# Filter tables of the later layers on VectorE, a merged score product for the first query tile, and an order from measured durations

## The chip, the cores and the metric

The kernel runs on one core of a Trainium2 chip. The metric is the device time of one execution in microseconds (us), the median of three runs. The engines of the core work side by side, each through its own list of instructions in order, and wait for each other at semaphores: TensorE (PE: matmuls, and PEld: its weight loads), VectorE (DVE), ScalarE (ACT), GpSimd (POOL) and SyncE (SP, which here issues DMAs).

## What is computed

The input is 2048 tokens of 512 features (8 sequences of 256). Four residual blocks follow each other:

```python
x = x + attn_a(layernorm(x))   # 4 layers: norm, silu, long convolution with a
                               # complex exponential filter, norm, 64->256->64 MLP
x = x + ffn(layernorm(x))      # 512 -> 1792 -> 512, weights w * (su @ sv), silu gate
x = x + attn_b(layernorm(x))   # 32 query heads, 8 key heads of 128, causal, ALiBi
x = x + ffn(layernorm(x))
```

The filter of the convolution is a power series. It is computed as a rotation by an angle that grows with the position, held in tables of cosine and sine (`rot`), between which a running sum (a scan along time) is made:

```python
p = jnp.tanh(r) * jnp.exp(1j * jnp.angle(phazor_c))
prog = p[None, :] ** jnp.arange(L, dtype=jnp.float32)[:, None]
```

The attention of one key head and its four query heads is

```python
scores = jnp.einsum('bkgqd,bksd->bkgqs', qg, k) / math.sqrt(HD)
attn = jax.nn.softmax(scores + bias[None], axis=-1)   # bias: causal mask and slope * distance
```

## The kernel before

Everything is kept in float32 precision by splitting: a value is held as a high part in the reduced type `float32r` and a low part, the rest. A product is made of three matmuls (`PASSES`: high x high, high x low, low x high), in the helper `mm3`, whose matmul is line 624. All split products of the kernel therefore stand at line 624, and are told apart by the names of their tiles.

**Opening and first feed-forward block (phase 1).** The four blocks of 512 tokens ("stacks" s = 0 to 3) go through the four-layer convolution stack. Stack 0 is the lead: the feed-forward block can only begin with its result. One norm of a layer is a chain over all engines: `sq` (ScalarE), `var` (TensorE, line 1337), `eps` (VectorE, line 1183), `rstd` (GpSimd, `srstd`, line 810), `rtr` (TensorE, line 1346), `yn` (VectorE). Then `silu` (ScalarE, line 949), `ur` (VectorE, 1197) and `ui` (GpSimd, 818) multiply by cosine and sine, `zr` and `zi` are the scans (VectorE, 1208), `pr` (VectorE) and `pi` (GpSimd, 821) multiply by the tables again, and `conv` is TensorE's (1356, 1358). The projection into the stack is `proj` (line 1330), ahead of it `row`, `xT`, `xc` bring in and transpose the tokens. Folding steps prepare constants: `b1f` (line 1309), `boutf` (line 1314).

The tables are made by doubling: `turn k` (five instructions on GpSimd, lines 767 to 773) squares the rotation, and the table of 2^k positions becomes one of 2^(k+1). For layer 0 this is `tab0` on VectorE (lines 1092, 1094). For layers 1 to 3 it is `tabs` on GpSimd: three instructions (lines 790, 791, 793), for levels 0 to 4 all three layers in one, from level 5 (`TAB_EACH`) on each layer by itself, 14 tables in all. `ui` and `ur` of layer l wait for its tables.

The order of all instructions of phase 1 is made by a planner, `Steps.ordered`: each step has an engine, an expected duration in us, the steps that it needs, and an urgency (0 is the lead's). It places the step that can start first; up to 130 us (`PATIENT`) steps that would delay a lead step are held back. The last feed-forward block has an order of its own from the same planner (`order3`).

**Attention (phase 2).** 64 units, one for each of 8 key heads and 8 sequences, in the order written out in `order2`. A unit has four heads. TensorE computes the scores of the four heads (`sc`), then keys and values of the next unit (`kv`), transposes the probabilities of heads 0 and 1 (`pT`, line 1850), computes queries of the next unit (`q`), the product with the values (`at`), and so on. Scores of the first 128 queries reach 128 keys, those of the second 128 reach 256; both lie in one PSUM bank of 512 columns (`PART`: 0 to 128 and 128 to 384). VectorE adds the bias and takes the row extreme in one instruction (line 1758), ScalarE takes the exponential (1618), VectorE the reciprocal of its sum (`rsum`, 1765), GpSimd multiplies (1673). Each head's reciprocal stands behind the scores of the next head in VectorE's list. `biased` has two buffers, so that head n waits for the exponentials of head n-2. In the last unit of a key head, `alibi` (line 1708) makes the bias of the next one between the heads. In the first four units VectorE also does layer-norm statistics ahead of the scores; near the end one unit has four of them.

## Time and profile before

| | |
|---|---|
| three timed runs | 2542.87, 2538.52, 2543.79 us, median 2542.87 |
| the profiled execution | 2549.18 us, its span 2547.9 us, mean granted clock 0.981 |
| TensorE busy | 2481.8 us, 97% of the span |
| VectorE, ScalarE, GpSimd busy | 1284.1, 944.2, 669.1 us |
| chain of work that ended last | TensorE 95%, VectorE 2%, GpSimd 2%, ScalarE 1% |

The busy shares are means over stages that differ. TensorE's busy time counts overlapping instructions, so the pace of matmuls is read from start to start.

### The profile page before, as it was taken

What the parts mean: (1) busy time and instruction counts of PE and PEld (TensorE: products, weight loads), DVE (VectorE), ACT (ScalarE), POOL (GpSimd) and SP (SyncE); (2) the same over time, 40 slices, a digit from 0 to 9 for tenths busy, and PEclk for the clock granted to TensorE, in tenths of its full rate; (3) what the DMA queues carried; (4) which work ended last, traced back from release to release, by engine and by line L of the source; (5) the groups of instructions that cost most, each with busy time, mean ns of one, the idle gap of its engine ahead of it and who ended that gap; (6) DMA issues with size and microseconds to landing.
All of it is one profiled execution on the core that took longest, in us unless ns stands there. A gap on an engine that the chain in (4) does not pass through costs nothing.

```text
span 2547.9 us, 38721 instructions
## 1 busy us (share of the span) xinstructions
PE 2481.8 (97%) x13618; PEld 2100.3 (82%) x13618; DVE 1284.1 (50%) x3248; ACT 944.2 (37%) x2576; POOL 669.1 (26%) x1182
## 2 busy tenths in 40 slices
PE   5899999999899999999999999999999989999999
PEld 4577778888688888888888888888888868888887
DVE  6656532221376666666666666666666651212122
ACT  5533211111255544545445445454454421111111
POOL 6541110000133433434334334343343310000000
PEclk7899999999899999999999999999999989999999
DMA  5234445455200000100000001000000025555553
GB/s 156 75 128 172 176 149 196 179 195 198 77 26 1 19 24 1 42 1 17 26 1 23 21 1 43 1 18 26 1 17 26 1 84 188 208 198 196 192 215 149
DMA packets 45117, 220.95 MB, mean 87 GB/s; under 512 B 5560, under 2 KB 5688, under 8 KB 30592
## 3 DMA queue, kind: packets, MB, share of 16 engines
q1 hardware_dynamic: 43568, 217.02, 23.2%
q8 instruction: 112, 1.84, 0.3%
q10 hardware_dynamic: 1360, 1.46, 0.2%
q14 instruction: 77, 0.63, 0.1%
HBM read 192.25 MB, written 26.21 MB: 86 GB/s over the span
## 4 chain that ended last, share of the span: by engine, by line
PE 95%; DVE 2%; POOL 2%; ACT 1%; issue 1%; DMA 0%; ACTq 0%; DVEq 0%; POOLq 0%
PE psum L624 83%; PE psum L1850 3%; PE psum L1825 2%; PE psum L1346 1%; PE psum L1367 1%; PE psum L1805 1%; PE psum L1330 1%; PE psum L1247 1%; PE psum L1337 0%; PE psum L1232 0%; PE psum L1389 0%; PE psum L1379 0%; PE psum L1787 0%; POOL srstd L810 0%; PE psum L1356 0%
## 5 line engine op out<-in xcount | busy, mean ns | idle before, releaser
L624 PE MATMUL psum<-wkvq_h,axT_h 128*128 128x256 f32 (+1 forms) x1024 | 358.9, 350 | 1.5 <-DVE axT_l L1696 1.5
L624 PE MATMUL psum<-wkvq_h,axT_l 128*128 128x256 f32 (+1 forms) x1024 | 347.2, 339 | 0.0
L624 PE MATMUL psum<-wkvq_l,axT_h 128*128 128x256 f32 (+1 forms) x1024 | 346.3, 338 | 0.0
L1673 POOL TENSOR_SCALAR prob<-prob,rsum 128x128 f32<-128x128 f32 (+1 forms) x512 | 214.3, 432 | 445.1 <-DVE rsum L1765 438.2
L1618 ACT ACTIVATE prob<-biased,nmax 128x128 f32<-128x128 f32 (+1 forms) x512 | 226.2, 443 | 216.5 <-DVE nmax L1758 216.5
L624 PEld LDWEIGHTS psum<-wkvq_h,axT_l 128*128 128x128 f32 x1024 | 195.4, 191 | 22.8
L624 PE MATMUL psum<-wo_h,oT_h 128*128 128x512 f32 x512 | 213.0, 416 | 0.0
L624 PEld LDWEIGHTS psum<-wkvq_h,axT_h 128*128 128x128 f32 x1024 | 195.5, 191 | 18.1 <-issue 1.9
L624 PEld LDWEIGHTS psum<-wkvq_l,axT_h 128*128 128x128 f32 x1024 | 196.0, 191 | 16.8
L624 PE MATMUL psum<-wo_h,oT_l 128*128 128x512 f32 x512 | 201.7, 394 | 0.0
L624 PE MATMUL psum<-wo_l,oT_h 128*128 128x512 f32 x512 | 200.3, 391 | 0.0
L1024 DVE TENSOR_TENSOR db<-gateb,psum 128x512 f32<-128x512 f32 x56 | 38.5, 688 | 315.4 <-PE psum L624 302.9
L1758 DVE CUSTOM_DVE_ANT_0 biased<-psum,alibi 128x128 f32<-128x128 f32 (+1 forms) x512 | 162.1, 355 | 3.7 <-ACT prob L1618 1.2
L1603 ACT ACTIVATE squares<-psum 128x512 f32<-128x512 f32 x128 | 76.6, 598 | 232.7 <-PE psum L624 232.7
L1734 DVE TENSOR_REDUCE ss_q<-squares 128x4 f32<-128x512 f32 x128 | 87.8, 686 | 131.8 <-ACT squares L1603 131.1
L1024 DVE TENSOR_TENSOR da<-gatea,psum 128x512 f32<-128x512 f32 x56 | 38.5, 687 | 228.0 <-PE psum L624 225.5
L624 PE MATMUL psum<-kT_h,qT_h 128*128 128x128 f32 (+1 forms) x512 | 143.1, 279 | 1.5 <-DVE qT_l L1748 1.5
L624 PE MATMUL psum<-kT_l,qT_h 128*128 128x128 f32 (+1 forms) x512 | 143.2, 280 | 0.0
L624 PE MATMUL psum<-kT_h,qT_l 128*128 128x128 f32 (+1 forms) x512 | 142.7, 279 | 0.0
L1778 DVE TENSOR_TENSOR x<-x,psum 128x512 f32<-128x512 f32 x128 | 88.1, 688 | 102.9 <-PE psum L624 96.9
L1768 DVE TENSOR_TENSOR pT_l<-psum,pT_h 128x384 fp32r<-128x384 f32 x256 | 130.2, 550 | 7.5 <-ACT pT_h L1625 7.4
L1608 ACT ACTIVATE qT_h<-psum 128x512 fp32r<-128x512 f32 x128 | 77.2, 603 | 149.6 <-PE psum L1825 149.6
(336 smaller groups left out, 5880.8 us busy)
## 6 DMA issues: line engine op xcount, KB each, us to landing
wgu0b<-weff_gu SPq DMA_DIRECT2D x19, 1024.0 KB, 5.6
wgu1b<-weff_gu SPq DMA_DIRECT2D x19, 1024.0 KB, 5.6
wgu2b<-weff_gu SPq DMA_DIRECT2D x18, 1024.0 KB, 5.6
wgu2a<-weff_gu SPq DMA_DIRECT2D x14, 1024.0 KB, 5.6
wgu0a<-weff_gu SPq DMA_DIRECT2D x14, 1024.0 KB, 5.7
wgu1a<-weff_gu SPq DMA_DIRECT2D x14, 1024.0 KB, 5.6
stage<-in_wqkv SPq DMA_DIRECT2D x16, 768.0 KB, 4.3
stage<-in_ffn_w SPq DMA_DIRECT2D x14, 768.0 KB, 5.1
```

The lines of the kernel that those rows point to most:

```text
L624: ins = pe.matmul(out_ap, stat[a], mov[b], start=start and n == 0, stop=stop and n == last)
L1024: dve.tensor_tensor(F["d"][:], F["gate"][:, a % 2, :], psum[:, UP, :], ALU.mult).then_inc(d_done, 1)
L1603: act.activation(squares[:], psum[:, QB[b], :], ACT.Square).then_inc(q_sq, 1)
L1608: act.activation(qT[0][:, :, b * P:(b + 1) * P], psum[:, QB[b], :].rearrange("p (h c) -> p h c", h=GRP), ACT.Copy).then_inc(qT_hi, 1)
L1618: act.activation(prob[:, b, lo:hi], biased[:, b % 2, lo:hi], ACT.Exp, bias=nmax[:, b, t:t + 1], scale=-1.0, accum_out=esum[:, b, t:t + 1]) ...
L1673: pool.tensor_scalar(prob[:, b, lo:hi], prob[:, b, lo:hi], rsum[:, b, t:t + 1], 1.0, ALU.mult, ALU.mult).then_inc(prob_done, 1)
L1734: dve.tensor_reduce(ss_q[:, b, :], squares[:].rearrange("p (h d) -> p h d", h=GRP), AX.X, ALU.add).then_inc(q_ss, 1)
L1758: dve.tensor_tensor_reduce(biased[:, b % 2, lo:hi], psum[:, b, lo:hi], alibi[:, b, lo:hi], -1.0, 3e38, ALU.add, ALU.min, nmax[:, b, t:t + ...
L1768: dve.tensor_tensor(pT[1][:, b % 2, :], psum[:, b, 0:SC], pT[0][:, b % 2, :].bitcast(F32), ALU.subtract).then_inc(pT_lo, 1)
L1778: dve.tensor_tensor(x[:, tile, :], x[:, tile, :], psum[:, (1, WO)[b], :], ALU.add).then_inc(o_add, 1)
L1825: ins = pe.transpose(psum[:, QB[b], hd * P:(hd + 1) * P], q_tok[:, b, hd * HD:(hd + 1) * HD], ident[:])
L1850: ins = pe.transpose(psum[:, b, k * P:(k + 1) * P], prob[:, b, k * P:(k + 1) * P], ident[:])
```

## The change

Three edits are made together.

1. The tables of layers 1 to 3 are computed by VectorE instead of GpSimd: for the shared levels with the same three instructions, for a single layer with two (a product, and a fused multiply and add). Their semaphore is `tabs_dve` instead of `tab_pool`.
2. The scores of the first query tile: high keys and low keys now lie side by side (`kT_both`), and one matmul of 256 columns multiplies the high queries with both. Its two halves go to two places in the bank, columns 0 to 128 and 384 to 512. A second matmul adds low queries x high keys to the first half. VectorE adds the second half and the bias first (`low_bias`), and then uses this sum in place of the bias. The second query tile now comes first on all engines.
3. The planner's durations for phase 1 are changed to ones measured, and `boutf` may come only after the lead's projection, at lower urgency.

```diff
-                o.add(("xT", s, j), "pe", 0.45 * slow, ...
+                o.add(("xT", s, j), "pe", 0.9 if lead else 0.45 * slow, ...
-            pe_step(("proj", s, 0), 1.75, ...
+            pe_step(("proj", s, 0), 2.5 if lead else 1.75, ...
-                    o.add(("inv", 0, 2 * T + j // 2), "pool", 1.15 if T else 0.95, ...
+                    o.add(("inv", 0, 2 * T + j // 2), "pool", 1.7 if T else 1.1, ...
-                o.add(("turn", k, 0), "pool", 0.8 if k else 0.2, ...
+                o.add(("turn", k, 0), "pool", 1.0 if k else 0.2, ...
-                    o.add(("tabs", k, l), "pool", 0.5 + 0.0045 * (2 << k) * (1 if l else 3), [("turn", k, 0)] + (
-                        [("tabs", k - 1, l if k > TAB_EACH else 0)] if k else []), 3)
+                    o.add(("tabs", k, l), "dve", 0.5 + 0.0025 * (2 << k) if l else 0.65 + 0.015 * (1 << k), [("turn", k, 0)] + (
+                        [("tabs", k - 1, l if k > TAB_EACH else 0)] if k else []), 1 + l)
-            o.add(("b1f", 0, 0), "pe", 3.4, [(began, 9.0)], 1, ("bank", 1, "early"))
+            o.add(("b1f", 0, 0), "pe", 3.6, [(began, 9.7)], 1, ("bank", 1, "early"))
-            o.add(("boutf", 0, 0), "pe", 0.9, [(began, 14.0)], 1, ("bank", 1, "early"))
-            o.add(("fold", 5, 0), "dve", 0.7, [("boutf", 0, 0)], 1, None, ("boutf", 0, 0))
-            o.add(("fold", 6, 0), "act", 0.6, [("boutf", 0, 0)], 1)
+            o.add(("boutf", 0, 0), "pe", 2.0, [("proj", 0, 0)], 3, ("bank", 1, "early"))
+            o.add(("fold", 5, 0), "dve", 0.7, [("boutf", 0, 0)], 3, None, ("boutf", 0, 0))
+            o.add(("fold", 6, 0), "act", 0.6, [("boutf", 0, 0)], 3)
...
+        def dve_tables(k, layer):
...
+            dve.tensor_tensor(ta, crossed, pair, ALU.mult).then_inc(tabs_dve, 1)
+            if layer:
+                dve.wait_ge(tabs_dve, done + 1)
+                dve.scalar_tensor_tensor(out=new, in0=old, scalar=turn[:, 2, k, layer:layer + 1], in1=ta, op0=ALU.mult,
+                                         op1=ALU.add).then_inc(tabs_dve, 1)
+            else:
+                both = turn[:, 2, k, ls].rearrange("p (i l o) -> p i l o", i=1, o=1).broadcast_to([P, 2, nl, n])
+                dve.tensor_tensor(new, old, both, ALU.mult).then_inc(tabs_dve, 1)
+                dve.wait_ge(tabs_dve, done + 2)
+                dve.tensor_tensor(new, new, ta, ALU.add).then_inc(tabs_dve, 1)
...
-                    for t in range(STILES):
-                        lo, hi = PART[t]
-                        dve.tensor_tensor_reduce(biased[:, b % 2, lo:hi], psum[:, b, lo:hi], alibi[:, b, lo:hi], -1.0, 3e38,
-                                                 ALU.add, ALU.min, nmax[:, b, t:t + 1]).then_inc(biased_done, 1)
+                    if n >= 2:
+                        dve.wait_ge(biased_done, STILES * (n - 1))
+                    dve.tensor_tensor(low_bias[:, b % 2, :], psum[:, b, SC:SC + P], alibi[:, b, 0:P], ALU.add).then_inc(low_done, 1)
+                    dve.tensor_tensor_reduce(biased[:, b % 2, P:SC], psum[:, b, P:SC], alibi[:, b, P:SC], -1.0, 3e38,
+                                             ALU.add, ALU.min, nmax[:, b, 1:2]).then_inc(biased_done, 1)
+                    dve.wait_ge(low_done, n + 1)
+                    dve.tensor_tensor_reduce(biased[:, b % 2, 0:P], psum[:, b, 0:P], low_bias[:, b % 2, :], -1.0, 3e38,
+                                             ALU.add, ALU.min, nmax[:, b, 0:1]).then_inc(biased_done, 1)
...
-                    for t in range(STILES):
-                        lo, hi = PART[t]
-                        q_ = slice(t * P, (t + 1) * P)
-                        ins = mm3(psum[:, b, lo:hi], [((qT[0][:, b, q_], qT[1][:, b, q_]),
-                                                       (kT[0][:, 0:hi - lo], kT[1][:, 0:hi - lo]))])
-                    ins.then_inc(sc_mm, 1)
+                    mm3(psum[:, b, P:SC], [((qT[0][:, b, P:SEQ], qT[1][:, b, P:SEQ]), (kT[0], kT[1]))])
+                    apart = psum[:, b, :].rearrange("p (n c) -> p n c", c=P)[:, 0:SC // P + 1:SC // P, :]
+                    pe.matmul(apart, qT[0][:, b, 0:P], kT_both[:, :, 0:P], start=True, stop=False)
+                    pe.matmul(psum[:, b, 0:P], qT[1][:, b, 0:P], kT[0][:, 0:P], start=False, stop=True).then_inc(sc_mm, 1)
```

## Rows read from the trace of the kernel before

**Rows 1.** Busy us and instructions of each engine by stage, then clock, DMA share, GB/s

```profile
0.00:131.00 131.00, 93.55 (x525) 63.48 (x525) 82.20 (x187) 70.51 (x146) 85.37 (x162) 0.79 0.36 113
...
702.00:2050.00 1348.00, 1346.17 (x8258) 1195.04 (x8258) 860.17 (x2476) 659.54 (x2071) 509.71 (x923) 1.00 0.05 16
```

**Rows 2.** Timeline of TensorE, opening: start us, length us, what, [idle before, releaser]

```profile
16.95 2.07 PE L1314 MATMUL psum<-wout_sb,vec 64*128 64x512 f32 x2
...
35.49 1.08 PE L1322 MATMUL psum<-ident,xna 128*128 128x128 f32 x4 [9.55 <-ACT xna L921]
...
55.68 1.12 PE L1346 MATMUL psum<-ident,srstd 128*64 128x128 f32 x8 [3.16 <-POOL srstd L810]
```

**Rows 3.** Timeline of GpSimd, opening

```profile
22.38 0.20 POOL L767 TENSOR_TENSOR sm<-turn 128x4 f32<-128x4 f32 x1
...
23.03 0.22 POOL L773 TENSOR_SCALAR turn<-sm 128x4 f32<-128x4 f32 x1
...
39.13 0.72 POOL L821 TENSOR_TENSOR buf_b<-buf_a,rot 128x256 f32<-128x256 f32 x1
...
54.61 1.01 POOL L810 TENSOR_TENSOR srstd<-svar,mneg_half 128x4 f32<-128x4 f32 x1
```

**Rows 4.** Instructions on `rot` alone, 18 to 55 us: VectorE, GpSimd, clock, DMA

```profile
18.00:55.00 37.00, 5.11 (x18) 19.93 (x44) 0.70 0.29 109
```

**Rows 5.** Timeline of ScalarE and VectorE, opening

```profile
27.50 0.60 ACT L949 ACTIVATE buf_e<-buf_d,vec 128x256 f32<-128x256 f32 x1
...
32.62 0.48 DVE L1094 SCALAR_TENSOR_TENSOR rot<-rot,turn,gatea 128x256 f32<-128x256 f32 x1
...
33.14 0.42 DVE L1197 TENSOR_TENSOR buf_c<-buf_e,rot 128x256 f32<-128x256 f32 x1
...
33.70 0.75 DVE L1208 TENSOR_TENSOR_SCAN buf_d<-sm,buf_c 128x256 f32<-128x256 f32 x1
...
51.55 0.16 DVE L1183 TENSOR_SCALAR svar<-psum 128x4 f32<-128x4 f32 x1 [0.18 <-PE psum L1337]
```

**Rows 6.** Timeline of TensorE in an ordinary attention unit, from 1240.52 us

```profile
1240.52 0.22 PE L624 MATMUL psum<-kT_h,qT_h 128*128 128x128 f32 x1
...
1241.20 0.22 PE L624 MATMUL psum<-kT_h,qT_h 128*128 128x128 f32 x1
...
1243.26 0.28 PE L624 MATMUL psum<-wkvq_h,axT_h 128*128 128x256 f32 x1
...
1246.13 0.82 PE L1850 MATMUL psum<-ident,prob 128*128 128x128 f32 x6
...
1249.56 0.39 PE L624 MATMUL psum<-pT_h,v_h 128*128 128x512 f32 x1
```

**Rows 7.** Timeline of TensorE in a unit with `alibi`, which starts at 1197.89

```profile
1203.51 0.83 PE L1850 MATMUL psum<-ident,prob 128*128 128x128 f32 x6
...
1207.73 0.28 PE L624 MATMUL psum<-pT_l,v_h 128*128 128x256 f32 x1
1207.85 0.28 PE L624 MATMUL psum<-pT_h,v_l 128*128 128x256 f32 x1
```

**Rows 8.** Timeline of VectorE, GpSimd and ScalarE in the ordinary unit

```profile
1241.40 0.29 DVE L1758 CUSTOM_DVE_ANT_0 biased<-psum,alibi 128x128 f32<-128x128 f32 x1
...
1241.62 0.42 DVE L1758 CUSTOM_DVE_ANT_0 biased<-psum,alibi 128x256 f32<-128x256 f32 x1
...
1242.09 0.29 DVE L1758 CUSTOM_DVE_ANT_0 biased<-psum,alibi 128x128 f32<-128x128 f32 x1
...
1243.03 3.45 POOL L1673 TENSOR_SCALAR prob<-prob,rsum 128x128 f32<-128x128 f32 x8 [7.30 <-DVE rsum L1765]
...
1246.33 0.28 ACT L1587 ACTIVATE squares<-psum 128x128 f32<-128x128 f32 x1 [0.98 <-PE psum L624]
...
1247.65 1.02 DVE L1768 TENSOR_TENSOR pT_l<-psum,pT_h 128x384 fp32r<-128x384 f32 x2
```

**Rows 9.** Timeline of GpSimd in the unit with `alibi`

```profile
1202.91 0.83 POOL L1673 TENSOR_SCALAR prob<-prob,rsum 128x128 f32<-128x128 f32 x2 [0.57 <-DVE rsum L1765]
```

## What I expect of the change, before it is run

> **What bounds the kernel now.** I read the busy time by stage first [rows 1]. The attention stage, 702 to 2050 us, holds 53% of the span and has TensorE busy for 1346.2 of 1348 us. The opening, 0 to 131 us, is loose: TensorE is busy 93.6 us of it. So the change can act in two places: where it takes TensorE work out of the full attention stage, and where it shortens the idle opening. Next I read the timeline of each engine in both places, to see who waits last there.
>
> In the opening the first stack (s = 0, the "lead") is a chain over all engines, and feed-forward can't begin before it ends. TensorE has two large holes in it: 9.55 us before 35.49 and 3.16 us before 55.68, the second put down to `srstd` on GpSimd [rows 2]. GpSimd's own timeline shows why: it works through the filter tables without a pause, so that `pi` begins only at 39.13 and the `srstd` of the second layer at 54.61 [rows 3].
>
> In attention the reader is to see a pitch, not a duration: the start of one matmul to the start of the next. One head's scores take 1241.20 - 1240.52 = 0.68 us for six matmuls, and matmuls of 256 columns start 0.12 us apart [rows 6, 7]. The busy times of 0.22 to 0.33 us overlap and say nothing of the pace.
>
> **Scores on TensorE.** Before: three products of 128 columns and three of 256. After: three of 256, one of 256 (high query against high and low keys side by side), one of 128. The columns stay 1152; one matmul and one weight load go. At 0.12 us each the three of 256 take 0.36 of 0.68, so the three of 128 take 0.32, 0.107 each: half the columns for nearly the same time. After: 4 x 0.12 + 0.107 = 0.587, which saves 0.68 - 0.587 = 0.093; over 24 matmuls (2.74 us from 1240.52 to 1243.26) it is 0.686 - 0.587 = 0.099. I take 0.10 us a head, 0.40 a unit. The new product writes two pieces of 128 columns, 384 apart. The `pT`/`v` product already writes a 256-column result in two strided pieces, at a pitch of 0.12 [rows 7]; so the form costs nothing there. Bounds: no saving, if columns set the pace, and 0.114 if every matmul costs a sixth of 0.686.
>
> A rule of the skill speaks against this part. The Trainium skill, "TensorE: Matmul & The Clock Gate", section "Back-to-back issue gap", gives an isolated gap of N/2.4 + 2.5 ns at the high clock, that is 56 ns for 128 columns and 109 for 256. By it a head would go from 495 to 492 ns, and the attention stage would gain under 1 us from it (the whole sum would be some -3 us). The same section gives about 81 ns for 128 columns in streams with a weight load for each matmul; with 109 for 256 that would save 53 ns a head, 13.6 us in 256 heads (the whole sum about -14). The trace agrees with its 109 for 256 to within a tenth, but with neither figure for 128.
>
> **Scores on VectorE.** It gains one instruction per head: `low_bias`, a 128x128 addition from PSUM. The nearest row is the 128x128 `biased` instruction, also from PSUM: 0.29 us, the next one starting 0.22 us later [rows 8]. A head takes 1242.09 - 1241.40 = 0.69 now; I take 0.90. The wait on `low_done` lies behind the 256-column instruction, whose 0.42 us cover it. Upper bound 0.42, the 128x256 size with nothing overlapped. Behind VectorE wait the exponentials on ScalarE, then `rsum`, the normalisation on GpSimd, and TensorE's transposes `pT`.
>
> Is that hidden? In an ordinary unit (starting at 1240.52) VectorE starts the first head at 1241.40, late because the residual addition is before it. The exponentials now take 0.9 us a head on ScalarE; they begin 0.38 later and each head takes 1.0 at most, so they end some 0.5 later than now. There ScalarE idled 0.98 us before it could square the new keys, at 1246.33 [rows 8]. TensorE reaches that point 0.40 earlier, so 0.58 of the idle time is left, just enough for 0.5. `pT` for the first head comes at 1246.13, which becomes 1245.73. The first head's probabilities are now due from GpSimd at 1243.03 + 3.45/4 = 1243.89, the second's at 1244.75 [rows 8]; two or three extra instructions make the second 0.42 later, 1245.17, with `pT` for it at 1246.0. So nothing waits: 0.40 us gained. This holds for 44 ordinary units and the 7 that follow a change of group.
>
> In the 7 units with `alibi` between the heads it does not hold. GpSimd ends the second head at 1202.91 + 0.83 = 1203.74, and TensorE transposes six tiles from 1203.51, the second three from about 1203.8 [rows 7, 9]: no slack. Before the second `rsum` stand three heads' scores, so it is 3 x 0.21 = 0.63 later, and TensorE stalls until then. These units get 0.6 us longer instead of 0.4 shorter. Six more units (the first four, whose heads stand behind layer-norm work, one near the end with the same, and the last, which has no `kv` work to cover) I set at no change. Attention: 51 x -0.40 + 7 x 0.6 = -16.2 us. Bounds: with 0.114 a head and no alibi stall, 58 x -0.46 = -27; with 0.07 a head and twice the stall, 51 x -0.28 + 7 x 1.2 = -6.
>
> **Tables on VectorE.** GpSimd loses 14 tables of three instructions: 19.93 us in 44 instructions, less `ui` and `pi` at 0.72 each, is 18.5 us [rows 3, 4]. VectorE gets them in 33 instructions (three for each of the five shared tables, two for each of nine single ones). Its 16 instructions for layer 0 took 5.11 less `ur` and `pr` at about 0.43 each, 4.25 us, 0.27 each; the widest took up to 0.48 [rows 4, 5]. More of the new ones are wide, so 33 x 0.30 = 10 us. Bounds 33 x 0.27 = 9 and 33 x 0.48 = 16.
>
> The lead gains this. Silu ends at 28.10 [rows 5]. A turn is five instructions on GpSimd in 0.87 us (22.38 to 23.25) [rows 3]. With no tables between them the four turns from 22.38 on and one `srstd` of 1.0 are done by 26.9, and the last `tab0` pair (0.9 us) before Silu ends. So `ur` can start at 28.15 instead of 33.14; 0.42 for `ur`, two scans of 0.75 each, and `pi` starts at about 30.2 instead of 39.13: 8.9 us. `srstd` of the next layer waited from 51.71 to 54.61: 2.9. `boutf` on TensorE (16.95, 2.07 us) leaves the place ahead of the first projection; the projection's inputs are due during it, so not all of it counts, and I take 1.2 [rows 2]. Together 13.0 us.
>
> Against it: VectorE must do 10 us of tables, plus the weight splits and folds that it did in the same stretch, before the second layer's `ur`, now some 12 us earlier. It idled 131 - 82.2 = 49 us in the opening, but not all where needed, and it is in order: a table of 0.9 us in front of a lead step delays the chain. I give back 3 of 13. A lead that ends 10 us sooner is not 10 us of span, since TensorE used part of that time for the other stacks, which it must now do later. The share that was idle bounds this: 37.4/131 = 29% of 10 is 3, all of it 10; the two holes (12.7 us) are wholly idle, so I lean to the upper side and take -7. The re-made order (other durations for `xT`, `proj`, `inv`, `turn`, `b1f`) can shift any step by a few us; I can't price it and set it at 0, with +-5.
>
> **Sum.** -16.2 - 7 = -23.2 us. The profiled execution took 2549.2 us, its span 2547.9; that becomes 2526.0. The three timed runs have a median 6.3 us lower, so I forecast 2542.9 - 23.2 = 2519.7, about 2520 us. The third order, of the last feed-forward block, has none of its costs changed, and I set it at nothing.
>
> **Rivals.**
> A. Columns set the pace, and one matmul less saves nothing. For it: the 256-column pitch of 0.12 is near what its columns need. Against: 128 columns take 0.107. Attention then has only its stalls, +4; with the opening -3: 2540 us. It is the Trainium skill's isolated-gap rule that gives this outcome. Chance 8%.
> B. The opening gives nothing or loses: VectorE's tables stand ahead of lead steps, or the new order is worse. Half of the added 10 us in the chain and a hole of some us at another place make it +5, so 2542.9 - 16.2 + 5 = 2532. For it: VectorE carries scans, row scalings and weight splits of the lead there. Against: 49 us idle. Chance 17%.
> C. Slower: VectorE becomes the pace of attention. Place: the new addition and its wait on `low_done`. If they take d instead of 0.21, the exponentials end about 4(d - 0.21) later; ScalarE's remaining 0.1 and TensorE's cover up to the `v` product (1249.56 against 1248.67 for `pT_l` [rows 6, 8], 0.9 less the 0.4) are gone at d = 0.36, and the 0.40 gained is gone at about d = 0.46. At d = 0.6 the 51 units lose 0.5 each, the 7 alibi ones 1.8: 2542.9 - 7 + 38 = 2574. Against: the row of 0.29. Chance 4%.
> My forecast with its own range, 2510 to 2528, has 68%; 3% is left for what I don't see.
>
> **Numbers.** A measurement of this kernel tells about 0.2%, 5 us, from no change. The range reaches from both parts good (-27 and -10: 2506) to B with a weak attention gain: 2506 to 2538. Faster by over 0.2%: forecast, B, and most of the rest: 88%. Within: A, 7%. Slower: C, 5%.
>
> **What would show it.** The start of a head's scores to the next is 0.59 us, not 0.68; `low_bias` costs VectorE about 0.21 a head; TensorE waits on `prob` in the alibi units only, 1.0 us each (0.6 and the 0.4 it came early); ordinary units have 20.8 us instead of 21.2. In the opening the hole before 35.49 shrinks to about 5 us, `pi` of the first layer starts near 30, and the first feed-forward matmul comes near 121 instead of 131. The prediction is wrong if the head's pitch stays at 0.68, if ordinary units wait for `prob` or `pT_l`, or if the feed-forward start doesn't move.

## The result, and the profile after

The changed kernel takes 2516.6 us (median of 2513.86, 2512.14, 2521.93 and 2519.31) against 2543.3 us (2538.52 to 2544.14) of the kernel before, measured side by side: a ratio of 0.990, 95% interval 0.9874 to 0.9925. The forecast was 2520.

The profiled execution after took 2513.86 us, its span 2512.5. I compare three stages with those of before: up to the first score matmul of attention, attention, and the rest. Attention starts at 691.69 instead of 702.20 (-10.5), lasts 1345.26 instead of 1365.67 (-20.4), and the rest takes 475.6 instead of 480.0 (-4.4). The sum, -35.3, is more than the medians' -26.7, because the profiled execution of before lay 5.9 us above its median and that of after 2.7 below; how much of each stage is not the change's is worked out below from further executions.

First the busy time by stage (columns as in [rows 1]):

```profile
0.00:131.00 131.00, 97.69 (x570) 67.83 (x571) 93.38 (x225) 72.82 (x151) 71.97 (x125) 0.91 0.36 113
...
702.00:2050.00 1348.00, 1330.61 (x8043) 1175.43 (x8042) 902.86 (x2742) 668.52 (x2071) 508.98 (x927) 1.00 0.06 18
```

VectorE has 11.2 us more in the opening and GpSimd 13.4 less; in attention VectorE has 42.7 us more. Next TensorE's timeline of the opening, against [rows 2]:

```profile
16.50 3.57 PE L1320 MATMUL psum<-vec,w_sb 64*128 64x1 f32 x16
20.00 3.68 PE L1341 MATMUL psum<-stack_xT,win_c 128*64 128x256 f32 x16
...
28.04 2.07 PE L1325 MATMUL psum<-wout_sb,vec 64*128 64x512 f32 x2
31.93 1.09 PE L1333 MATMUL psum<-ident,xna 128*128 128x128 f32 x4 [1.82 <-ACT xna L900]
...
46.38 1.12 PE L1357 MATMUL psum<-ident,srstd 128*64 128x128 f32 x8 [0.93 <-POOL srstd L789]
...
120.63 0.47 PE L625 MATMUL psum<-xT0ha,wgu0a 128*128 128x512 f32 x1
```

The hole of 9.55 us is 1.82 now, the 3.16 us for `srstd` are 0.93, that matmul comes 9.3 us sooner, and feed-forward begins at 120.63 instead of 131.09. `b1f` now stands directly ahead of the projection, where `boutf` stood before. The output of the lead's stack, which in the kernel before is

```profile
112.20 3.78 PE L1389 MATMUL psum<-wout_sb,buf_e 64*128 64x512 f32 x8 [0.61 <-DVE buf_e L1189]
```

is in the changed kernel

```profile
104.79 1.99 PE L1400 MATMUL psum<-wout_sb,buf_e 64*128 64x512 f32 x8 [0.61 <-DVE buf_e L1200]
```

so of the 10.5 us the lead itself brings 7.4, and 3.1 come between its output and the first feed-forward matmul. GpSimd's timeline, against [rows 3]:

```profile
29.53 0.97 POOL L797 TENSOR_TENSOR buf_b<-buf_e,rot 128x256 f32<-128x256 f32 x1 [1.27 <-ACT buf_e L928]
31.76 0.83 POOL L800 TENSOR_TENSOR buf_b<-buf_a,rot 128x256 f32<-128x256 f32 x1 [1.27 <-DVE buf_a L1219]
...
44.81 1.51 POOL L789 TENSOR_TENSOR srstd<-svar,mneg_half 128x4 f32<-128x4 f32 x1 [3.77 <-DVE svar L1194]
```

`pi` starts at 31.76 instead of 39.13, and each of these steps has a wait for another engine in its brackets: here GpSimd is no longer who comes last. VectorE's timeline shows what came in its place, and what `ur` now waits for:

```profile
29.49 0.42 DVE L1208 TENSOR_TENSOR buf_c<-buf_e,rot 128x256 f32<-128x256 f32 x1 [0.38 <-ACT buf_e L928]
30.05 1.00 DVE L1219 TENSOR_TENSOR_SCAN buf_d<-sm,buf_c 128x256 f32<-128x256 f32 x1
...
39.94 1.37 DVE L1095 SCALAR_TENSOR_TENSOR rot<-rot,turn,gatea 128x256 f32<-128x256 f32 x1
41.35 2.08 DVE L1165 TENSOR_TENSOR long_st<-long_raw,long_st 32x896 fp32r<-32x896 f32 x2
...
44.18 0.48 DVE L1183 TENSOR_SCALAR h<-psum,vec_c 128x256 f32<-128x256 f32 x1
```

`ur` waits for ScalarE's Silu, not for tables. The lead's `h` of the next layer, whose product TensorE had done at about 42.4, stands behind tables and weight splits.

In an ordinary attention unit (starting at 1224.11) TensorE shows the new pace, against [rows 6]:

```profile
1224.11 0.40 PE L625 MATMUL psum<-kT,qT_h 128*128 128x256 f32 x2
1224.35 0.28 PE L625 MATMUL psum<-kT,qT_l 128*128 128x256 f32 x1
1224.47 0.28 PE L1861 MATMUL psum<-kT,qT_h 128*128 128x256 f32 x1
1224.59 0.22 PE L1862 MATMUL psum<-kT,qT_l 128*128 128x128 f32 x1
1224.65 0.46 PE L625 MATMUL psum<-kT,qT_h 128*128 128x256 f32 x2
...
1229.33 0.82 PE L1867 MATMUL psum<-ident,prob 128*128 128x128 f32 x6
```

A head's scores start 1224.65 - 1224.11 = 0.54 us apart here, and over four heads (`kv` starts 2.30 us into the unit, before 2.74) the mean is 0.575. `pT` comes 5.22 us into the unit without a wait. VectorE and ScalarE in the same unit, against [rows 8]:

```profile
1224.92 0.28 DVE L1772 TENSOR_TENSOR low_bias<-psum,alibi 128x128 f32<-128x128 f32 x1
1225.12 0.41 DVE L1773 CUSTOM_DVE_ANT_0 biased<-psum,alibi 128x256 f32<-128x256 f32 x1
...
1225.46 0.29 DVE L1776 CUSTOM_DVE_ANT_0 biased<-psum,low_bias 128x128 f32<-128x128 f32 x1
...
1225.67 0.29 DVE L1772 TENSOR_TENSOR low_bias<-psum,alibi 128x128 f32<-128x128 f32 x1
...
1230.85 1.02 DVE L1786 TENSOR_TENSOR pT_l<-psum,pT_h 128x384 fp32r<-128x384 f32 x2
```

```profile
1229.54 0.28 ACT L1601 ACTIVATE squares<-psum 128x128 f32<-128x128 f32 x1 [0.23 <-PE psum L625]
```

`low_bias` takes 1225.12 - 1224.92 = 0.20 us of VectorE, a head 0.75 here. ScalarE still idles 0.23 us before the squares (0.98 before): the cover holds, with that left. Of the waits of TensorE within attention, the kernel before had four for `prob`, and none for `xn_a`:

```profile
PE psum L1850 <- POOL prob L1673: 1.9, 4, 0.8
```

The changed kernel has eleven and three (us in total, number, longest):

```profile
PE psum L1867 <- POOL prob L1687: 7.4, 11, 1.6
PE psum L625 <- DVE pT_l L1786: 2.9, 2, 1.7
PE psum L1805 <- DVE xn_a L966: 2.3, 3, 0.8
```

Seven of the eleven are new, those of the `alibi` units. Two are in unit 60, which has four layer-norm steps ahead of its heads, and two in the last unit; these four were there before, and are longer now. The three for `xn_a`, 0.78 us each, are those of units 1 to 3. The waits for `pT_l` are both in the last unit, and were there before.

### The profile page after: what moved, and what is told of

Read it like the earlier page. It is cut to its first block, busy times and chain, and to the rows that moved or that the text cites. A ratio compares the mean times of both kernels' runs of the same rounds, so it can differ in the third digit from the quotient of the medians.

```text
span 2512.5 us, 38710 instructions
## 1 busy us (share of the span) xinstructions
PE 2444.9 (97%) x13362; PEld 2067.6 (82%) x13362; DVE 1323.6 (53%) x3537; ACT 949.4 (38%) x2576; POOL 645.7 (26%) x1140
## 4 chain that ended last, share of the span: by engine, by line
PE 92%; DVE 3%; ACT 1%; issue 1%; POOL 1%; DMA 0%; SPq 0%; DVEq 0%; ACTq 0%; POOLq 0%
PE psum L625 80%; PE psum L1867 3%; PE psum L1843 2%; PE psum L1861 1%; PE psum L1357 1%; PE psum L1378 1%; PE psum L1823 1%; PE psum L1258 1%; PE psum L1390 1%; PE psum L1862 1%; ACT prob L1632 0%; PE psum L1348 0%; DMA short_raw<-in_lr_short 0%; PE psum L1243 0%; POOL srstd L789 0%
## 5 line engine op out<-in xcount | busy, mean ns | idle before, releaser
L1632 ACT ACTIVATE prob<-biased,nmax 128x256 f32<-128x256 f32 (+1 forms) x512 | 227.6, 446 | 236.1 <-DVE nmax L1773 236.1
L625 PEld LDWEIGHTS psum<-wkvq_l,axT_h 128*128 128x128 f32 x1024 | 195.8, 191 | 16.2
L1681 POOL TENSOR_TENSOR r_q<-ss_q,mneg_half 128x4 f32<-128x4 f32 x128 | 128.9, 1007 | 10.6
L1791 DVE TENSOR_TENSOR oT_l<-psum,oT_h 128x512 fp32r<-128x512 f32 x128 | 88.5, 691 | 57.4 <-ACT oT_h L1644 57.4
L625 PE MATMUL psum<-kT,qT_h 128*128 128x256 f32 x512 | 113.5, 303 | 1.5 <-DVE qT_l L1762 1.5
L1867 PE MATMUL psum<-ident,prob 128*128 128x128 f32 x768 | 107.3, 274 | 7.4 <-POOL prob L1687 7.4
```

What stands on the lines that cost most here:

```text
L625: ins = pe.matmul(out_ap, stat[a], mov[b], start=start and n == 0, stop=stop and n == last)
L1632: act.activation(prob[:, b, lo:hi], biased[:, b % 2, lo:hi], ACT.Exp, bias=nmax[:, b, t:t + 1], scale=-1.0, accum_out=esum[:, b, t:t + 1]) ...
L1681: pool.tensor_tensor(r_q[:, b, :], ss_q[:, b, :], mneg_half[:, 0:GRP], ALU.pow).then_inc(q_rs, 1)
L1791: dve.tensor_tensor(oT[1][:, hs, :], psum[:, 2 * b, :].rearrange("p (h c) -> p h c", h=2), oT[0][:, hs, :].bitcast(F32), ALU.subtract).the ...
L1867: ins = pe.transpose(psum[:, b, k * P:(k + 1) * P], prob[:, b, k * P:(k + 1) * P], ident[:])
```

## The experiments

Beside every median stands the ratio to the kernel before, run on the same chip, with its 95% interval. "Attention" is the stage from the first score matmul to the last output matmul of the profiled execution, "first FFN" the start of the first feed-forward matmul. "Ordinary unit" is the length that most of these units have.

| run | median us | ratio | first FFN | attention starts | attention lasts | ordinary unit |
|---|---|---|---|---|---|---|
| before | 2543.3 | 1 | 131.1 | 702.2 | 1365.7 | 21.18 |
| changed | 2516.6 | 0.990 [0.9874, 0.9925] | 120.6 | 691.7 | 1345.3 | 20.70 |
| scores only | 2525.1 | 0.9936 [0.992, 0.9952] | 131.0 | 703.0 | 1348.0 | 20.78 |
| tables only | 2533.2 | 0.9959 [0.9944, 0.9974] | 119.8 | 692.2 | 1359.4 | 21.10 |
| order only | 2538.1 | 0.9981 [0.9968, 0.9995] | 122.5 | 690.5 | 1362.0 | 21.10 |
| all but scores | 2531.5 | 0.9958 [0.9946, 0.997] | 124.1 | 695.1 | 1363.0 | 21.18 |
| six matmuls | 2542.1 | 1.0008 [0.9999, 1.0017] | 119.4 | 690.4 | 1368.4 | 21.09 |
| low_bias twice | 2533.2 | 0.9971 [0.9959, 0.9983] | 122.7 | 693.7 | 1358.2 | 20.70 |
| alibi spread | 2515.2 | 0.9904 [0.989, 0.9918] | 126.1 | 697.2 | 1341.4 | 20.70 |
| changed, again | 2515.3 | 0.9907 [0.9893, 0.9921] | 122.0 | 693.0 | 1345.3 | 20.70 |
| b1f as before | 2515.5 | 0.9902 [0.9887, 0.9917] | 123.1 | 693.0 | 1345.2 | 20.70 |
| all spread | 2511.7 | 0.9881 [0.9864, 0.9897] | 124.4 | 695.4 | 1337.9 | 20.70 |
| layer norm behind rows | 2507.5 | 0.9854 [0.9834, 0.9874] | 122.6 | 693.6 | 1334.5 | 20.70 |

The last four columns show one execution each, and it isn't always near the median of its run: 2532.2 us for scores only (median 2525.1), 2529.4 for order only (2538.1, over ten executions from 2529.4 to 2544.7), 2540.2 for all but scores (2531.5). What a part is worth is therefore taken from the ratios, and the stages tell where it lies.

### The parts by themselves

**Scores only**: the kernel before with the score part of the diff (`low_bias`, `kT_both`, `TILE_ORDER` and the merged product) and nothing else.

> The merged score product alone; tables on GpSimd and the old order, as in the kernel before. If the two parts add: attention gets 19 us shorter (ordinary units 20.7 instead of 21.2 us), the opening stays as before (first feed-forward matmul at 131 us), about 2524 us. Rival, that the parts help each other (an earlier feed-forward start changes what attention meets): attention gains under 15 us here.

-16.3 us by the ratio; the attention stage is 17.7 shorter (19 was expected) and the opening unmoved (131.03).

**Tables only**: `dve_tables` with the planner told of it, all other durations and `boutf` as before.

```diff
-o.add(("tabs", k, l), "pool", 0.5 + 0.0045 * (2 << k) * (1 if l else 3), ..., 3)
+o.add(("tabs", k, l), "dve", 0.5 + 0.0025 * (2 << k) if l else 0.65 + 0.015 * (1 << k), ..., 1 + l)
```

> The tables on VectorE alone, with their own new planner duration and urgency; all other durations and the place of boutf old, scores old. If GpSimd's tables were what held the lead, the first feed-forward matmul comes 8 to 10 us before 131 and the kernel takes about 2534 us. Rival, that the re-made order (boutf later, b1f after the first transposes) brought most of the 10.5: under 4 us here, about 2540.

-10.4 us, and feed-forward begins 11.3 us sooner (119.8). TensorE's timeline has no wait for `srstd` at the second layer, whose matmul comes at 48.93 instead of 55.68, and the big hole is still 6.64 us long:

```profile
31.62 1.09 PE L1332 MATMUL psum<-ident,xna 128*128 128x128 f32 x4 [6.64 <-ACT xna L899]
...
48.93 1.12 PE L1356 MATMUL psum<-ident,srstd 128*64 128x128 f32 x8
```

**Order only**: the new durations and the later `boutf`, with the tables left on GpSimd.

> The new durations and the later boutf alone; tables on GpSimd with their old duration, scores old. By the theory of the tables: 1 to 3 us sooner at the first feed-forward matmul, about 2541 us, since ui, pi and srstd still wait for GpSimd's tables. By the rival, that the order brought most: 7 or more sooner, about 2535.

-4.8 us, between the theory (about 1) and the rival (about 7); the profiled execution, the fastest of its ten, had feed-forward 8.6 us sooner (122.5), as the rival says. It gets `pi` to 35.42 by another road: GpSimd's timeline has it ahead of most of the single tables.

```profile
35.14 0.32 POOL L793 TENSOR_TENSOR rot<-rot,gatea 128x64 f32<-128x64 f32 x1
35.42 0.72 POOL L821 TENSOR_TENSOR buf_b<-buf_a,rot 128x256 f32<-128x256 f32 x1
...
37.46 0.29 POOL L790 TENSOR_TENSOR gatea<-rot,turn 128x64 f32<-128x64 f32 x1
```

The tables then stand before the second layer instead, and TensorE waits there:

```profile
53.13 1.12 PE L1346 MATMUL psum<-ident,srstd 128*64 128x128 f32 x8 [3.89 <-POOL srstd L810]
```

**All but scores**:

> Everything except the score part: tables on VectorE and new durations. The opening as in the changed kernel (first feed-forward matmul near 121 us), attention as before: 10.5 us less, about 2533. If the saving is not carried to the end (given back in the first feed-forward block), attention would begin less than 10 us before 702.

-10.7 us, no more than the tables alone: the two opening parts overlap. With the scores' -16.3 the sum is -27.0, against -25.4 for the whole by its ratio: the score part and the opening part add up.

### What the score part gains and costs

**Six matmuls**: the changed kernel with its merged product taken apart, so that VectorE keeps the extra addition and TensorE gets its sixth matmul back.

```diff
-pe.matmul(apart, qT[0][:, b, 0:P], kT_both[:, :, 0:P], start=True, stop=False)
+pe.matmul(psum[:, b, SC:SC + P], qT[0][:, b, 0:P], kT[1][:, 0:P], start=True, stop=True)
+pe.matmul(psum[:, b, 0:P], qT[0][:, b, 0:P], kT[0][:, 0:P], start=True, stop=False)
```

> The changed kernel, but the 256-column product of the first query tile is made as two of 128 columns into the same places: six matmuls a head, VectorE's work, tile order and the opening as in the changed kernel. If one weight load less is the gain: a head's pitch goes back from 0.58 to 0.69 us, ordinary units to about 21.15, and 58 units lose 0.45 each: +25 us against the changed kernel, about 2542. Rival, that the gain comes from the new order of the tiles or VectorE's new form and the number of columns sets the pace: under 5 us.

The whole gain goes (2542.1). TensorE's timeline has the same columns in six matmuls:

```profile
1232.60 0.28 PE L625 MATMUL psum<-kT,qT_l 128*128 128x256 f32 x1
1232.71 0.23 PE L1861 MATMUL psum<-kT,qT_h 128*128 128x128 f32 x1
1232.78 0.27 PE L1862 MATMUL psum<-kT,qT_h 128*128 128x128 f32 x1
1232.88 0.27 PE L1863 MATMUL psum<-kT,qT_l 128*128 128x128 f32 x1
1233.00 0.45 PE L625 MATMUL psum<-kT,qT_h 128*128 128x256 f32 x2
```

Head to head it is 1233.00 - 1232.31 = 0.69 us, and the ordinary unit 21.09 instead of 20.70: 0.39 for four matmuls with their weight loads. It also shows VectorE's addition without the gain. Against tables only, which has the old scores, ordinary units are no longer (21.09 and 21.10 us), but the `alibi` units are 0.41 longer each, units 1 to 3 0.48 and unit 60 0.41: the addition costs 4.7 us in the units that have no slack. Attention as a whole is 9.0 longer (1368.4 against 1359.4), because another 4.8 lie in the first and the last unit, where TensorE's granted clock was lower (0.83 against 0.89, and 0.75 against 1.00), and of the 23.1 us against the changed kernel 3.8 lie there.

**low_bias twice**: a second, unused addition of the same size ahead of `low_bias` in every head, into a tile of its own.

```diff
+dve.tensor_tensor(low_twin[:, b % 2, :], psum[:, b, SC:SC + P], alibi[:, b, 0:P], ALU.add)
 dve.tensor_tensor(low_bias[:, b % 2, :], psum[:, b, SC:SC + P], alibi[:, b, 0:P], ALU.add).then_inc(low_done, 1)
```

> The changed kernel with a second copy of the low_bias addition per head, into a tile that nobody reads: 0.20 us more on VectorE a head, 0.41 in all. If the cover ends at some 0.36, as I worked out before the result, ordinary units get 0.1 to 0.3 us longer and those with alibi 0.6: +10 to +18 us. If instead the slack seen in the new trace holds (ScalarE idle 0.23 us before it squares the keys, then 0.9 us before the product with the values), ordinary units don't change and only the 7 with alibi, the first few and one near the end get 0.6 longer each: +6 to +8 us.

The median rises by 17.9 us over the changed kernel's second run, but not where I had put the danger: ordinary units stay at 20.70. Units after a change of group get 0.18 longer, `alibi` units 0.7 (21.5 to 22.21), units 1 to 3 0.5 to 0.9, units 4 and 5 0.5, which makes 9 us. Attention is 12.8 longer: unit 60 is 1.8 longer and the last one 2.4, but at granted clocks of 0.93 and 0.76, where the changed kernel had 1.00 and 0.91, so that most of these 4.2 us can't be put down to the edit. The last stage was 4.4 longer in the same profile, which the edit doesn't explain either (below).

**Alibi spread**: the `alibi` steps of the next group, which stood between the heads of the group's last unit, are put one by one into VectorE's gaps later in that unit.

```diff
-                if b == BATCH - 1 and nxt:
-                    order2.append(("alibi", g + 1, hd))
...
             order2.append(("norm", u, GRP - 1))
+            bias_next = [("alibi", g + 1, hd) for hd in range(GRP)] if b == BATCH - 1 and nxt else []
+            order2 += bias_next[0:1]
```

The other three follow behind `qsc` of the first tile, behind the first `qT`, and ahead of the last `out`.

> The changed kernel with the four alibi instructions of a group's last unit moved on VectorE from between the heads to after them: one after the last reciprocal, one after each scaling of the queries' and the key tile's low parts, one ahead of the residual addition. If TensorE's wait on prob in these units comes from alibi standing between the heads, the 7 units go from 21.55 to about 20.8 us and the kernel gains 5 us over the changed one. Rival, that the wait moves into the new places (v_l, qT_l or the first scores of the next group, which need it): no gain.

Seven of the eleven waits for `prob` are gone (TensorE's waits in attention):

```profile
PE psum L1870 <- POOL prob L1690: 3.5, 4, 1.6
```

The units fall from 21.5 to 20.78, that is 0.7 each, though the wait removed was only 0.55 each: idle time is counted from the end of the last matmul's record, which overlaps the next start. From start to start the second head's transposes came 0.71 us later in the changed kernel than here. The seven units gain 5.2 us together. The attention stage is only 3.9 shorter, since unit 60, in which nothing was moved, took 24.65 us at a granted clock of 0.93 (23.15 at 1.00 in the changed kernel's second run), and the last unit 0.7 more at 0.82. And the median doesn't show the 5 us expected: 2515.2 against 2515.3. The profiled execution had the slowest opening of all (first FFN 126.1), but the other three, at 2513.3 to 2515.2, are no faster than the changed kernel's best either. The gain is shown in the units, not in the time of the kernel.

**Changed, again**, for a second execution under the profile:

> The changed kernel once more, beside the others on the same chip. Its spread tells what a difference is worth: 2512 to 2522 us. If the last feed-forward block was 5.9 us shorter only because the granted clock did not fall at its start, this stretch differs between runs of the same kernel (473 or 479 us).

Attention repeats to 0.1 us; the opening is 1.4 later.

### The order of the opening

**b1f as before**: in the changed kernel the two figures of this step are put back.

```diff
-o.add(("b1f", 0, 0), "pe", 3.6, [(began, 9.7)], 1, ("bank", 1, "early"))
+o.add(("b1f", 0, 0), "pe", 3.4, [(began, 9.0)], 1, ("bank", 1, "early"))
```

> The changed kernel with the duration and time of the b1f step as before (3.4, 9.0), so that the b1f matmuls stand ahead of the lead's transposes again; nearly the whole opening's order is made anew by it. Theory that the order alone put the projection later: the projection starts at 18.9 to 19.3 instead of 20.0, the rest of the lead follows it by 0.5 to 1 us at most, and the first FFN matmul is at 118 to 122; nothing to be seen in the median (2513 to 2519). Rival: the opening follows the granted clock between 60 and 90 us and not this order; the projection is sooner by 1 us, but the first FFN matmul is anywhere in 119 to 126, by the clock of that stretch.

The matmuls of `b1f` are first again, and the projection starts at 19.73, later than the 18.9 to 19.3 expected:

```profile
11.18 3.57 PE L1320 MATMUL psum<-vec,w_sb 64*128 64x1 f32 x16 [6.87 <-DMA b_sb<-in_b]
14.68 3.86 PE L1333 MATMUL psum<-ident,xna 128*128 128x128 f32 x16
19.73 3.33 PE L1341 MATMUL psum<-stack_xT,win_c 128*64 128x256 f32 x16 [1.19 <-DVE win_c L1121]
```

It now waits for `win_c`, which VectorE's re-made order brings at 19.25 instead of 17.31, so this run doesn't tell what the place of `b1f` alone is worth. With the changed kernel's own order, which eight executions share (changed; changed, again; all but scores; six matmuls; low_bias twice; alibi spread; all spread; layer norm behind rows), the projection started between 18.08 and 20.00, and what decides is the pace of `b1f` ahead of it. In four executions its sixteen matmuls took 3.57 us and the projection started at 19.27 to 20.00; in the other four they took 1.9 to 2.2 us and it started at 18.08 to 18.54. From the changed kernel's second run:

```profile
16.20 1.94 PE L1320 MATMUL psum<-vec,w_sb 64*128 64x1 f32 x16
18.08 1.95 PE L1341 MATMUL psum<-stack_xT,win_c 128*64 128x256 f32 x16
```

The granted clock reads 1.00 from 16 to 20 us in all eight, so it doesn't tell why the pace differs; the cause stays open.

### A faster version

**All spread**: as "alibi spread", and the layer-norm steps of units 0 to 3 go behind the heads, the four of unit 60 into the same four places.

```diff
-            if u < TPB:
-                order2.append(("ln", (2, NT - TPB + u), 1))
...
-            if u == UNITS - 4:
-                order2 += [("ln", (3, 0), TPB), ("inv", 3, 0), ("load", 0, 1)]
...
+            if u < TPB:
+                order2.append(("ln", (2, NT - TPB + u), 1))
+            if u == UNITS - 4:
+                bias_next = [("ln", (3, j), 1) for j in range(TPB)]
+            order2 += bias_next[0:1]
```

> As the run with the alibi steps behind the heads, and also each layer-norm step of VectorE in the attention stage behind the unit's heads (units 0 to 3), and the four of the fourth-last unit spread over that unit. Waiting-for-prob theory (a VectorE step ahead of the heads is paid by TensorE as soon as VectorE's head is no longer shorter than GpSimd's pace allows): units 1 to 3 fall from 22.6 to 21.7, the length of units 4 and 5; the fourth-last unit from 23.1 to 24.6 down to 20.7 to 21.5; the alibi units stay at 20.8 instead of 21.5. The attention stage is 1345.3 - 5.2 - 3 - 2 = 1335 us against 1345.3 of the changed kernel, and the median about 2506 to 2510. Rival: these units are long for another reason (the projection transposes and the clock at the start of the stage, the weight loads at its end), so they stay within 0.2 us and the attention stage is 1340 to 1342 as in the run with the alibi steps alone; the median is 2512 to 2518.

Unit 60 falls from 23.1 to 20.70 and the `alibi` units to 20.70, but units 1 to 3 stay at 22.5. The median is above the 2506 to 2510 expected, and attention, at 1337.9, lies between the theory (1335) and the rival (1340 to 1342). TensorE's timeline of unit 2 says why:

```profile
748.78 0.66 PE L1812 MATMUL psum<-ident,xn_a 128*128 128x128 f32 x4 [0.66 <-DVE xn_a L966]
```

The releaser is not `prob` but `xn_a`, and VectorE's timeline shows what stood ahead of it, the layer-norm step itself:

```profile
747.39 0.67 DVE L956 BATCH_NORM_STATS2 ln_bn<-x 128x6 f32<-128x512 f32 x1
...
748.20 0.53 DVE L966 TENSOR_SCALAR xn_a<-x,ln_mv,ln_rstd 128x512 f32<-128x512 f32 x1
```

**Layer norm behind rows**: so this step goes behind the second rows step, ahead of its transposes.

> As the run with all steps spread, but the layer-norm step of units 0 to 3 behind the second of VectorE's rows steps, before the second projection transposes, instead of ahead of the first. In that run TensorE still waited 0.66 us for xn_a in units 1 to 3, because the layer-norm step (0.81 us) stood between the last norm and the rows step that writes xn_a. Waiting-for-xn_a theory: units 1 to 3 fall from 22.5 to 21.7, the attention stage from 1337.9 to 1335.4, the median by 2 to 3 us, which 4 or 5 runs can just not tell from no change: 2508 to 2512. Rival: the layer-norm step only moves the wait to the second xn_a or to pT_l, and the units stay above 22.2; the stage is 1337 to 1338.

Units 1 to 3 are at 21.7, the length of units 4 and 5. The transposes follow without a wait:

```profile
745.40 0.66 PE L1812 MATMUL psum<-ident,xn_a 128*128 128x128 f32 x4
```

Attention lasts 1334.5 us, 10.7 less than in the changed kernel: 5.5 in the `alibi` units, 2.7 in units 1 to 3 and 2.4 in unit 60. The median is 2507.5, range 2502.49 to 2509.3, the fastest version here. The runs were made on different chips, so the ratios are compared: 0.9854 [0.9834, 0.9874] against 0.990 and 0.9907 [0.9893, 0.9921] of the changed kernel. The last step by itself is shown by units 1 to 3 alone (2.4 us together): the intervals of this run and of all spread overlap, and of the 3.4 us between their attention stages another 1.8 lie in the last unit, at a granted clock of 0.91 against 0.75.

## Why the prediction was right, point by point

**The sum.** -23.2 was forecast, the medians have -26.7. One profile pair gives -35.3, but its parts can be checked against the other executions of the same stages. Attention: four with the old scores have a mean of 1362.5 us, four with the new ones and the old places of `alibi` and layer norm (changed; changed, again; `b1f` as before; scores only) 1346.0: -16.6, forecast -16.2. Start of attention: 702.2 and 703.0 with the old opening; with the changed one eight executions between 690.4 and 697.2, mean 693.8: -8.8, forecast -7. Together -25.4. The profile pair's further 4.4 us are in the last stage, which the change doesn't touch (below). The attention term was right piece by piece; the opening term came out near its figure partly by luck (below).

**The matmul that goes.** Right: 0.098 us a head by the six-matmul run (0.39/4), forecast 0.10. Over the 51 units with slack, the two runs that differ in this alone differ by 19.3 us, 0.095 a head. Rival A, that columns set the pace, is dead. The Trainium skill, "TensorE: Matmul & The Clock Gate", section "Back-to-back issue gap", differs from this: by its isolated gaps (56 and 109 ns) a head would have gained 3 ns, by its 81 ns for 128 columns in streams with weight loads, with the isolated 109 for 256, 53 ns. The measured 98 decides.

**The units.** The unit lengths, in us:

| units | before | forecast | after |
|---|---|---|---|
| 42 ordinary | 21.10 to 21.21 | -0.40 | 20.70 to 20.81 |
| 4 and 5, counted as ordinary | 22.01 | -0.40 | 21.70 |
| 7 after a change of group | 21.41 to 21.48 | -0.40 | 21.01 to 21.07 |
| 7 with `alibi` | 21.15 | +0.6 | 21.5 |
| 1 to 3 | 22.1 to 22.4 | 0 | 22.6 |
| 60 | 22.66 | 0 | 23.07 |

The `alibi` mechanism was right: VectorE's scores make the second head's `prob` late. Its size was too large: a stall of 1.0 us was forecast, and from start to start it is 0.71 (the waits in the trace are 0.54 to 0.63 us). The units with layer norm ahead of their heads were the small miss: I set them at no change, and units 1 to 3 and 60 lose 0.4 each, 1 to 3 at the new wait for `xn_a`. By the means of the two fours, the 51 units give -20.8 (forecast -20.4), the `alibi` units +2.8 (+4.2), units 1 to 3 and 60 +1.8 (0), the first and the last unit -0.4 (0).

**VectorE's addition.** 0.20 us a head, forecast 0.21. That an ordinary unit hides it was right, and two runs bear it out: the unit is 20.70, and at twice the cost still 20.70. So the point from which rival C decides, d = 0.36, was too low for these units. The step that failed is "0.9 less the 0.4": I let TensorE's `v` product come 0.4 sooner and left `pT_l` where it was. But `pT_l` hangs on TensorE's own transposes and came sooner with it (1230.85 - 1224.11 = 6.74 us into the unit, before 1247.65 - 1240.52 = 7.13), so the slack is still 0.88. The other part was mis-sized too: ScalarE had 0.23 us of idle time left, not 0.1, since its exponentials end 0.35 us later in the unit than before and not 0.5. At twice the cost they end another 0.52 later, not 4 x 0.20 = 0.8; ScalarE's idle time is gone, and `pT_l` starts only 0.19 later, which leaves 0.69 of slack. What does break at twice the cost are the units without slack.

**The opening.** What held the lead was named rightly: GpSimd's tables held up `pi` and `srstd`. The sizes were not, and -7 against -8.8 is partly two errors that cancel. The 8.9 us of `pi` were 7.4 in the profile pair: the first scan took 1.00 us, not 0.75, and Silu began 1.3 later. It began later because the term of 1.2 for the projection failed: `boutf` left the place ahead of it, but the changed order put `b1f` there, and the projection came 1.05 later (20.00 against 18.95), at `b1f`'s slower pace; in the four executions with the faster one it came 0.4 to 0.9 sooner. The 2.9 for `srstd` were 1.9: from `pi` to the second layer's `srstd` matmul it is 14.6 us instead of 16.6, and the rest is spent in VectorE's queue, where `h` stands behind splits, and in the `srstd` instruction itself (1.51 us against 1.01). VectorE's tables took 11.0 us (forecast 10). I expected the lead to end 10 us sooner and 7 of them to count. In the pair it was 9.3 sooner at the second layer and 7.4 at its output, so the later layers gave some back; on the mean of the eight executions it was 5.3 at the output (106.9 against 112.2). All of it counted, and 3.1 us came on top from a term that I had set at 0: between the lead's output and the first feed-forward matmul every re-made order has 15.1 to 16.2 us, and the old order 18.9, with the projection of the last stack directly ahead of feed-forward there.

**Which opening part did it.** Not fully settled. Tables alone give -10.4 and the order alone -4.8 by medians, both together -10.7, while in single profiles the order alone looked as good (690.5). That they overlap is shown; how the 10 us divide is not, since one opening varies by 7 us in attention's start. Nor was the part of the new durations separated from that of the later `boutf`.

**Rival B** (the opening gives nothing) is refuted by the run of all but scores, whose interval excludes 1.

## What to carry to other kernels

Where small matmuls follow each other with a weight load each, count matmuls and not columns, and take the price from the start-to-start pace of the trace: here merging two 128-column products into one saved 0.1 us each time, and one more VectorE addition was free as long as its followers had slack. Then look for the few units where they have none: a step that stands ahead of a chain in an in-order queue and could as well stand behind it (bias tables, layer norm) cost 0.7 us in each such unit with bias tables, 0.9 in those with one layer-norm step and 2.4 in unit 60, and moving all of them took 10.7 us more out of the attention stage. A moved step must clear all chains, though: behind the first it stood in front of the next, until the releaser in the wait's brackets was read again.

## What the runs showed of the hardware that was not expected

**One opening, many times.** Eight executions with the changed opening had their first FFN matmul between 119.4 and 126.1 us. The granted clock between 60 and 90 us was 0.89 in the two fastest (119.4, 120.6), 0.83 in the next (122.0, 122.7), and 0.66 in the four others (122.6, 124.1, 124.4, 126.1). The windows view of this stretch in the changed kernel (columns as in [rows 1]):

```profile
60.00:90.00 30.00, 23.36 (x153) 15.17 (x149) 21.95 (x41) 20.97 (x45) 16.04 (x20) 0.89 0.66 226
```

The same in the slowest, alibi spread:

```profile
60.00:90.00 30.00, 26.02 (x135) 16.56 (x131) 19.90 (x34) 18.57 (x40) 13.13 (x16) 0.66 0.56 193
```

There is more busy time for fewer matmuls at the lower clock. But `b1f` as before had 0.90 and came at 123.1, so the clock there is not the whole of it. Whether it is the cause of a late opening or follows from TensorE's idle time was not tried.

**The same at the last block.** In the profile of before the clock at the start of the last feed-forward block was 0.76 and 0.90 in two stretches of 20 us:

```profile
2060.00:2080.00 20.00, 15.63 (x58) 12.12 (x57) 12.07 (x25) 4.16 (x6) 2.57 (x6) 0.76 0.40 159
```

At the same place of the changed kernel it was 1.00 in both, with the same busy time and more matmuls:

```profile
2030.50:2050.50 20.00, 15.61 (x79) 12.14 (x78) 13.48 (x28) 5.57 (x9) 3.04 (x6) 1.00 0.40 159
```

With the same code for this stage it took 475.6 us in four executions (changed; changed, again; order only; `b1f` as before), 478.4 in one (alibi spread) and 479.8 to 480.8 in the eight others. In single profiles this 4.4 us looks like a gain or a loss of the change.

**Two paces of one unit.** Ordinary units of the same code took 21.10 us or 21.18, and 20.70 or 20.78, at a granted clock of 1.00. The longer pace holds for whole groups of eight units: in the changed kernel for one group, in its second run for another one, in scores only for all but the first. The cause is not known. With all groups it would be some 3.5 us.

**The ends of the attention stage.** The last unit took 17.2 us in two executions (tables only, all but scores) at a granted clock of 1.00, 18.2 to 18.6 in six at 0.91, and 20.0 in the profile of before at 0.74. This is 1.5 us of that profile's -20.4, and with the two paces it explains most of the difference between -20.4 and -16.6.
